# Causal attention: the probabilities' transpose by an identity becomes a product with a diagonal of inverse sums

## The reference, cut to what matters

```
q = einsum('qdh,bcd->bhcq', Q, x) * sq
k = einsum('qdh,bcd->bhcq', K, x) * sq
v = einsum('vdh,bcd->bhcv', V, x) * sv
att = einsum('bhcq,bhCq->bhcC', q, k) / 64          # then causal mask
p = softmax(att, axis=-1)
y = einsum('bhcC,bhCv->bhcv', p, v)
z = einsum('dvh,bhcv->bcd', W, y) * (sqrt(256 / 64) / 16)
x = layernorm(x + z)
```

## Time and profile before

| | |
|---|---|
| median of 3 runs | 2179.88 us (2178.33 to 2181.05) |
| profiled execution, its own time | 2181.41 us |
| its span, first to last instruction | 2179.6 us |
| PE (matmul) busy | 1758.3 us, 81% |
| DVE busy | 1469.8 us, 67% |
| ACT busy | 992.0 us, 46% |
| POOL busy | 500.8 us, 23% |

### The profile page before, as it was taken

One profiled execution on the slowest core, in us unless ns is written; L12 is line 12 of the kernel. 1 busy time (PEld: TensorE's weight loads), 2 busy tenths in 40 slices (PEclk: granted clock), 3 DMA queues, 4 the chain that ended last, 5 costly groups with the idle time before them and its releaser, 6 DMA issues.

```text
span 2179.6 us, 34541 instructions
## 1 busy us (share of the span) xinstructions
PE 1758.3 (81%) x12713; PEld 1265.2 (58%) x12713; DVE 1469.8 (67%) x5012; ACT 992.0 (46%) x2312; POOL 500.8 (23%) x602
## 2 busy tenths in 40 slices
PE   3546666766677877999999999999888999998808
PEld 1335555655564335566666766666657999983306
DVE  3788887787822587677777567776735666753695
ACT  2524334443343753455555345555315445543762
POOL 3011112111120012333333333333302333320002
PEclk9767788878787986999999999999999999999959
DMA  5000000000000011100000000000403333310001
GB/s 153 1 0 1 1 1 1 1 1 1 1 1 1 1 39 24 60 1 1 1 1 1 1 1 2 1 1 2 128 1 88 88 88 78 70 30 0 0 0 39
DMA packets 86314, 49.82 MB, mean 23 GB/s; under 512 B 40205, under 2 KB 83905, under 8 KB 85953
## 3 DMA queue, kind: packets, MB, share of 16 engines
q1 hardware_dynamic: 79361, 47.05, 8.3%
q10 hardware_dynamic: 6784, 0.56, 0.3%
HBM read 45.50 MB, written 2.10 MB: 22 GB/s over the span
## 4 chain that ended last, share of the span: by engine, by line
PE 60%; DVE 19%; ACT 9%; issue 3%; POOL 3%; POOLq 0%; DVEq 0%; ACTq 0%
PE PS L1526 6%; PE PS L1553 6%; PE PS L1824 5%; PE PS L1540 5%; PE PS L713 3%; PE PS L1511 3%; PE PS L1501 3%; DVE sq L667 3%; DVE nx L664 3%; PE PS L719 3%; PE PS L2237 3%; PE PS L1887 2%; PE PS L1568 2%; PE PS L1843 2%; PE PS L1493 2%
## 5 line engine op out<-in xcount | busy, mean ns | idle before, releaser
L1680 POOL TENSOR_SCALAR px<-px,crl 128x128 f32<-128x128 f32 (+7 forms) x128 | 225.9, 1765 | 420.6 <-DVE crl L1652 420.6
L1591 ACT ACTIVATE px<-PS,cnm 128x128 f32<-128x128 f32 (+7 forms) x256 | 189.5, 741 | 265.3 <-DVE cnm L1637 258.5
L182 POOL TENSOR_SCALAR rstd<-mv 128x1 f32<-128x1 f32 x128 | 41.5, 325 | 794.3 <-DVE mv L161 793.6
L667 DVE TENSOR_SCALAR sq<-nx 128x4 f32<-128x4 f32 x1024 | 186.0, 182 | 35.3 <-DVE nx L664 0.2
L664 DVE TENSOR_TENSOR_SCAN nx<-sq 128x6 f32<-128x6 f32 x1024 | 176.2, 172 | 35.5 <-SPq L2304 2.3
L1634 DVE TENSOR_REDUCE cm<-PS 128x1 f32<-128x128 f32 (+6 forms) x224 | 154.2, 689 | 56.9 <-PE PS L1526 56.4
L1540 PE MATMUL PS<-ident,px 128*128 128x128 f32 x1152 | 159.8, 280 | 13.3 <-ACT qT L1579 9.6
L1540 PEld LDWEIGHTS PS<-ident,px 128*128 128x128 f32 x1152 | 131.2, 142 | 60.6 <-issue 35.3
L1526 PE MATMUL PS<-kT,qT 64*128 64x512 f32 (+3 forms) x768 | 158.9, 519 | 4.5 <-ACT px L1591 2.6
L1553 PEld LDWEIGHTS PS<-pT,V 128*64 128x64 f32 x2304 | 124.1, 137 | 64.0 <-issue 34.6
L1553 PE MATMUL PS<-pT,V 128*64 128x128 f32 x2304 | 154.1, 278 | 6.4 <-DVE pT L1645 2.8
(11 more groups left out here) (318 smaller groups left out, 3830.3 us busy)
## 6 DMA issues: line engine op xcount, KB each, us to landing
xbs<-in_fside_Bx16xSxS SPq DMA_DIRECT2D x8, 1232.0 KB, 6.6
fsrc<-in_fside_Bx16xSxS SPq DMA_DIRECT2D x8, 1232.0 KB, 6.6
xmk<-in_mask_Bx16xSxS_bk SPq DMA_DIRECT2D x8, 308.0 KB, 8.5
fsrc<-in_mask_Bx16xSxS_bk SPq DMA_DIRECT2D x8, 308.0 KB, 8.3
X<-in_x SPq DMA_DIRECT2D x1, 2048.0 KB, 11.8
w<-in_L_attn_W_ffn SPq DMA_DIRECT2D x2, 1024.0 KB, 11.9
t<-in_L_ffn_w SPq DMA_DIRECT2D x2, 1024.0 KB, 11.3
out<-xs SPq DMA_DIRECT2D x16, 128.0 KB, 1.7
```

The costliest lines, as they stand in the source:

```text
L667: e.tensor_scalar(o, bass.AP(k.nx, 2, [[6, P], [0, 2], [3, 2]]), 10.0, -10.0, ALU.min, ALU.max).then_inc(sem("rec.clip"), 1)
L1591: e.activation(k.px[n % 2][:, h, 0:width], src, ACT.Exp, scale=-1.0, bias=k.cnm[:, n % 4, h:h + 1], accum_out=k.cl[:, n % 4, h:h + 1]).the ...
L1680: e.tensor_scalar(k.px[n % 2][:, 0, 0:width], k.px[n % 2][:, 0, 0:width], k.crl[:, n % 4, 0:1], None, ALU.mult).then_inc(sem("c.normal0"), 1)
```

## The change

The normalisation no longer touches px. DVE multiplies the identity by the inverse sums of a head, into a new tile `diag[n%2][:, h, :]` of 128x128, and `ct` multiplies each px block by that diagonal instead of transposing it by the identity; the product is the transposed block with its queries scaled. POOL's `cn` is gone, head 0's blocks come first, and the copies of pT alternate between DVE and ACT.

```diff
@@ causal_tiles
+    k.diag = [sb(f"diag{s}", [P, 2, P], scope=inner) for s in range(2)]
@@ causal_order
-                by = min(sum(made) % 3, 1)
+                by = sum(made) % 2
@@ causal_groups
-    blocks = [(h, j) for h in (1, 0) for j in range(qt + 1)]
+    blocks = [(h, j) for h in range(2) for j in range(qt + 1)]
@@ causal_tensor
     def ct(u, qt):
         ring = (at("cs", u, qt) - 1) % 2
-        w.wait_ge("c.normal1", at("cs", u, qt))
+
+        w.wait_ge("c.normal0", at("cs", u, qt))
         for i, group in enumerate(causal_groups(qt)):
             bank, name, value = k.room["ct", u, qt, i]
             w.wait_ge(name, value)
             for q, (h, j) in enumerate(group):
-                if h == 0:
-                    w.wait_ge("c.normal0", at("cs", u, qt))
-                y = e.transpose(PS[:, bank, q * P:(q + 1) * P], k.px[ring][:, h, j * P:(j + 1) * P], k.ident[:, :])
+                if h:
+                    w.wait_ge("c.normal1", at("cs", u, qt))
+                y = e.matmul(PS[:, bank, q * P:(q + 1) * P], k.px[ring][:, h, j * P:(j + 1) * P], k.diag[ring][:, h, :], start=True, stop=True, skip_group_check=True)
             y.then_inc(sem("c.turn"), 1)
@@ causal_tensor, cp
-                y = e.matmul(PS[h * 64:(h + 1) * 64, 6, qt % 4 * P:(qt % 4 + 1) * P], k.V[s][:, j, h * 64:(h + 1) * 64], k.pT[ring][:, (1 - h) * (qt + 1) + j, :],
+                y = e.matmul(PS[h * 64:(h + 1) * 64, 6, qt % 4 * P:(qt % 4 + 1) * P], k.V[s][:, j, h * 64:(h + 1) * 64], k.pT[ring][:, h * (qt + 1) + j, :],
@@ causal_vector
     def cn(u, qt, h):
+
         n = at("cs", u, qt) - 1
-        width = (qt + 1) * P
-        w.wait_ge("c.normal0", n - 3)
         w.wait_ge("c.exp", 2 * n + h + 1)
         e.reciprocal(k.crl[:, n % 4, h:h + 1], k.cl[:, n % 4, h:h + 1]).then_inc(sem("c.rl"), 1)
-        if h == 0:
-            return
-        w.wait_ge("c.rl", 2 * n + 2)
-        e.tensor_scalar(k.px[n % 2][:, 1, 0:width], k.px[n % 2][:, 1, 0:width], k.crl[:, n % 4, 1:2], None, ALU.mult).then_inc(sem("c.normal1"), 1)
+        w.wait_ge("c.rl", 2 * n + h + 1)
+        e.tensor_scalar(k.diag[n % 2][:, h, :], k.ident[:, :], k.crl[:, n % 4, h:h + 1], None, ALU.mult).then_inc(sem(f"c.normal{h}"), 1)
@@ causal_pool
-    def cn(u, qt, h):
-        if h:
-            return
-        n = at("cs", u, qt) - 1
-        width = (qt + 1) * P
-        w.wait_ge("c.rl", 2 * n + 1)
-        e.tensor_scalar(k.px[n % 2][:, 0, 0:width], k.px[n % 2][:, 0, 0:width], k.crl[:, n % 4, 0:1], None, ALU.mult).then_inc(sem("c.normal0"), 1)
-
-    return {"causal_setup": setup, "cn": cn}
+    return {"causal_setup": setup}
```

## The result

The changed kernel takes 2278.88 us (median of 4 runs, 2277.53 to 2279.36) against 2179.93: 98.95 us more, a ratio of 1.0453 with a 95% interval of 1.0435 to 1.0472. The forecast was 2281.

What follows compares the result with a forecast made beforehand. TensorE (PE), busy 96% of a 670 us stage, was taken as the bound. 2181.4 + 130.2 + 1 - 30.5 = 2282.1, and with that execution 1.5 us above the median, 2281 us; range 2270 to 2295.

Steps and rivals of the forecast that it cites:

- Two passes a product: In ct, an f32 product takes two passes, 0.223 us against 0.110 for a transpose: +130.2 us over 1152 blocks.
- the 1 us for entering: On TensorE, entering a run of products costs slightly more than entering transposes: +1 us for all runs.
- What is absorbed: Slower blocks on TensorE run into existing waits for DVE and ACT later, and other hidden time goes: -30.5 us together.
- The qT term: ct's third group at qt=4 no longer waits for ACT's qT copy; with two other waits ahead of L1540: -14.4 us.
- The slips: Inside runs of transposes, banks late by less than shows as idle no longer delay TensorE: -6.2 us over 16 units.
- The scores' and L1568's waits: At the stage's end the scores' waits for exp, and L1568's one wait, go behind longer blocks: -4.2 us.
- The pT term: Half of cp's waits for pT copies go, since the earlier copies no longer queue: -3.9 us.
- The last step: In the last unit the idling for px and the half-clock run behind it go, so the second pass is free: -1.8 us.
- DVE: DVE's diagonals, 0.28 us each, and extra copies cost nothing, DVE at 64%; rival: DVE becomes the wait, 2317 us, 5%.
- one pass a product: Rival: in ct the diagonal product costs one pass like the transpose, so not slower, about 2176 us; 3%.
- nothing absorbed: Rival: TensorE's waits move along with the later stages of the ring, so none is absorbed: 2311 us; 9%.
- four transposes a product: Rival: in ct a product holds PE for four transposes, 0.44 us a block: about 2530 us; 2%.

Runs made afterwards that it cites:

- the relief alone: The changed kernel with ct transposing px by the identity again, diagonals still made and waited for, normalisation left out of the result: 2180.24 us, ratio 1.0003.
- half, whole and double: Kernel before with px multiplied by the identity for head 1's blocks only, 2224.75 us, or all blocks, 2283.97; changed kernel with every product issued twice, 2533.28.
- the other order: The kernel before with the transposes of the previous step put ahead of this step's projections: 2258.58 us; the same edit on the changed kernel: 2307.42 us.
- the old split: The changed kernel with the copies of pT split as before, one in three on DVE and two on ACT: 2282.58 us, ratio 1.047.
- the product alone: The kernel before with ct multiplying px by the identity instead of transposing it, px still normalised by POOL and DVE: 2283.97 us, ratio 1.0476.
- bf16 with the other order: The changed kernel with px and the diagonals in bf16 and the transposes ahead of the projections: 2282.68 us, ratio 1.0475.

## Why the prediction was right, point by point

- **What bounds the stage**: right. PE at 96% before, 99.3% after, and the relief alone, with 226 us off POOL, is no faster than the kernel before.
- **Two passes a product**: right, 2304 records, 0.111 to 0.112 us each, 0.22 a product in the run with doubled products. +130.2 stands; with the 1 us for entering, 131.2.
- **What is absorbed**: forecast 30.5, measured 131.2 - 98.95 = 32.3. The curve of half, whole and double shows that it is absorption and not a lower price: 19.6, then 5.9, then 1.8. The sum came out better than its parts, as the next points show.
- **The qT term**, -14.4: its waits are gone, 9.6 us before and none after, and the row of 20 records above runs through. What they cost by themselves was to be measured by the other order, and that failed.
- **The slips**, -6.2: right. Runs of 24 and 28 records take 2.84 and 3.29 us after, which is their slots and one length.
- **The scores' and L1568's waits**, -4.2: the scores' wait for exp fell from 2.6 us to 0.2, but L1568's 1.1 us is there unchanged, as L1570's. About 2.7 of the 4.2 came.
- **The pT term**: I took half of 7.8 us, -3.9, and gave the reason that copies no longer queue, while I had costed the split of the copies at nothing. The idle time in the row of the P·V products fell by 1.7 us (6.4 to 4.7), and by only 0.6 with the old split (5.8). So the reason given accounts for little, part of what came is the split's, and the term was too large. That the split helps beside slow products and seems to harm beside transposes wasn't in the working at all.
- **The last step**: that the idling and the half-clock run would go is right. The term of -1.8 isn't shown to be the change's doing. The waiting is gone because px is ready: with px still normalised on POOL and DVE, 1.84 us of it stayed. But the lower clock doesn't follow from the waiting: after 1.84 us of it 32 records took 3.84 us in the product alone, and after the same 1.38 us the same 16 transposes took 2.04 us in the kernel before with the other order.
- **The first steps**: not in the working. Ahead of the window that I had read, one projection ran at the lower clock before and not after, which is 1.8 us of the absorption and made good part of what the two terms above lacked. The granted clock from 876 to 890 is 0.76 before and 1.00 after. As it is 0.76 with the doubled diagonals too, and 1.00 in the kernel before with the other order, it doesn't go with the change, and I count this as luck:

```profile
882.33 3.78 PE L1493 MATMUL PS<-XT,wqT 128*128 128x512 f32 x4
...
881.61 1.99 PE L1494 MATMUL PS<-XT,wqT 128*128 128x512 f32 x4
```

- **DVE**: right, 0.287 us a diagonal (0.28 taken), and 73.5 us more of it changed nothing.
- **The rivals**: one pass a product, out by the records; nothing absorbed, out by the curve; DVE, out by the doubled diagonal; four transposes a product, out by the doubled product (255 us where it asked for 507). On this the trace doesn't agree with the Trainium skill's page on TensorE (TensorE: Matmul & The Clock Gate, Terms), which has transpose mode four times as fast for FP32; here it is 0.110 against 0.223, twice as fast.

## What to carry to other kernels

Before work is folded into a matmul that stands in for a transpose, count the records of each in the trace against the instructions in the code: in f32 the product was two passes, the transpose one, and in a stage at 96% of TensorE every pass counted. Take busy time off an engine only where somebody waits for it. Here the first 65 us that were added to the bounding engine came out at 45.5, and of 62 taken from it 24 arrived, because they trade against its waits; half, whole and double of the edit show how much. A wait that a list shows as gone can live on in gaps too short for the list: compare the length of the stage and the idle time of the row too.

## What was not expected

- A product in float32r is one pass with a slot of 0.113 us, against 0.223 for float32 and 0.056 for bf16, at the same shape of 128x128 by 128.
- Projections between the scores and the transposes were cover, not filler: swapping two neighbours in the order cost 79 us, though the one wait aimed at went away.
- After 1.38 us of waiting in the kernel before, the granted clock fell to the lower level for the next 16 transposes. After the same wait in the other order it stayed at 1.00, and after 1.84 us in the product alone too. What decides between them is open.
- In bf16 with the other order PE's granted clock was 0.91 over the stage, so that the waits cost a second time, in slower work: 55 us beside 70 of idling.
